# Shared-expert work of two mixture-of-experts layers moved behind the routing chain and behind the expert slots

## What is computed

```python
# first mixture
shared = silu(x @ shared_w1.T) @ shared_w2.T
gates, idx = top_k(x @ gate_w.T, 2); gates = softmax(gates)
out = shared + sum over the two experts of gate * (silu(x @ w1[e].T) @ w2[e].T)
# second mixture
w, idx = top_k(softmax(x @ w_router), 2); w = w / (sum(w) + 1e-8)
out = sum over the two of w * ((silu(x @ w_gate[e]) * (x @ w_up[e])) @ w_down[e])
      + (silu(x @ ws_gate) * (x @ ws_up)) @ ws_down
```

## Time and profile before

| | us |
|---|---|
| median of 3 runs | 769.45 (768.46 to 769.53) |
| the profiled execution, its own time | 768.8 |
| its span in the trace | 767.1 |
| TensorE busy | 582.7 (76% of the span) |
| VectorE busy | 422.9 (55%) |
| ScalarE busy | 333.4 (43%) |
| GpSimd busy | 352.9 (46%) |
| attention, up to the last rows normed | 0 to 79.5 |
| routing 1, up to the first turn of a slot | 79.5 to 118.8 |
| slots of layer 0 | 118.8 to 243 |
| combine, norm, state space | 243 to 545 |
| routing 2, up to the first turn of a slot | 545 to 604 |
| slots of layer 1 | 604 to 738 |
| combine, norm, store | 738 to 767.1 |

### The profile page before, as it was taken

One profiled execution on the slowest core, in us unless ns is written; L12 is line 12 of the kernel. 1 busy time (PEld: TensorE's weight loads), 2 busy tenths in 40 slices (PEclk: granted clock), 3 DMA queues, 4 the chain that ended last, 5 costly groups with the idle time before them and its releaser, 6 DMA issues.

```text
span 767.1 us, 9002 instructions
## 1 busy us (share of the span) xinstructions
PE 582.7 (76%) x2522; PEld 345.9 (45%) x2523; DVE 422.9 (55%) x717; ACT 333.4 (43%) x594; POOL 352.9 (46%) x281
## 2 busy tenths in 40 slices
PE   6887798788786539849776975665699799999940
PEld 3755475566564213214323332221355566666630
DVE  3344471000011869999999999999376233222326
ACT  3433332444444275764883685343212144433423
POOL 1000215666653116676667668576100456556422
PEclk9998699999999679998998998999989899999985
DMA  4503001111111943423443343342000101111123
GB/s 110 171 25 137 15 4 42 36 39 41 40 34 50 359 195 130 144 113 137 143 149 109 137 151 133 117 150 82 15 0 1 32 29 41 35 38 33 31 81 92
DMA packets 35135, 65.61 MB, mean 86 GB/s; under 512 B 6111, under 2 KB 23207, under 8 KB 34464
## 3 DMA queue, kind: packets, MB, share of 16 engines
q1 hardware_dynamic: 29824, 51.19, 19.7%
q0 software_dynamic: 4992, 9.32, 4.6%
q10 hardware_dynamic: 288, 4.72, 1.6%
HBM read 57.60 MB, written 8.52 MB: 86 GB/s over the span
## 4 chain that ended last, share of the span: by engine, by line
PE 41%; issue 16%; POOL 14%; DVE 13%; another core or an unknown queue 6%; ACT 6%; DMA 3%; SPq 0%; POOLq 0%; ACTq 0%; DVEq 0%
PE ps L600 8%; PE ps L581 8%; DVE wide L1352 7%; POOL wide L1475 6%; POOL w L1475 6%; PE ps L583 4%; PE ps L537 3%; PE ps L592 3%; PE ps L693 3%; ACT work L937 3%; PE ps L502 2%; PE ps L506 2%; PE ps L507 2%; PE ps L635 1%
## 5 line engine op out<-in xcount | busy, mean ns | idle before, releaser
L1352 DVE TENSOR_TENSOR_SCAN wide<-work,ps 128x1024 f32<-128x1024 f32 x64 | 146.2, 2284 | 1.9
L937 ACT ACTIVATE work<-work,a_neg 128x512 f32<-128x512 f32 (+1 forms) x128 | 84.5, 712 | 103.2 <-DVE wide L1352 83.1
L1504 POOL DMA_INDIRECT y_choice<-yout,dest x78 | 78.8, 1011 | 98.3 <-ACT yout L758 71.9
L1475 POOL TENSOR_TENSOR wide<-wide,w 128x1024 f32<-128x1024 f32 x32 | 75.6, 2362 | 62.0 <-DVE wide L1352 62.0
L693 PE MATMUL ps<-w,ident 128*128 128x512 f32 x128 | 68.9, 669 | 33.4 <-POOL w L1475 33.4
L1475 POOL TENSOR_TENSOR w<-wide,w 128x1024 f32<-128x1024 f32 x32 | 78.4, 2454 | 32.0 <-DVE wide L1352 32.0
L1198 DVE COPY xT<-ps 128x128 f32<-128x128 f32 x78 | 22.7, 291 | 118.5 <-PE ps L575 62.3
L1345 DVE TENSOR_TENSOR ps<-ps,w 128x1024 f32<-128x1024 f32 x64 | 78.9, 1233 | 6.4
L693 PE MATMUL ps<-wide,ident 128*128 128x512 f32 x128 | 63.2, 617 | 21.5 <-POOL wide L1475 21.5
L1498 POOL DMA_INDIRECT xin<-xn_rows,source x40 | 39.2, 979 | 85.9 <-DVE dest L1173 74.3
L1203 DVE TENSOR_TENSOR wide<-wide,ps 128x512 f32<-128x512 f32 x39 | 26.8, 688 | 77.1 <-ACT wide L836 72.2
(11 more groups left out here) (234 smaller groups left out, 965.9 us busy)
## 6 DMA issues: line engine op xcount, KB each, us to landing
w<-bc_rows SPq DMA_DIRECT2D x64, 512.0 KB, 3.6
w<-in_w ACTq DMA_DIRECT2D x2, 2304.0 KB, 9.0
w<-y_choice SPq DMA_DIRECT2D x16, 256.0 KB, 3.7
wg<-in_wg SPq DMA_DIRECT2D x1, 2304.0 KB, 10.8
wu<-in_wu SPq DMA_DIRECT2D x1, 2304.0 KB, 15.8
wd<-in_wd SPq DMA_DIRECT2D x1, 2304.0 KB, 21.1
y_choice<-yout,dest POOLq DMA_INDIRECT x78
work<-in_x SPq DMA_DIRECT2D x4, 256.0 KB, 3.3
```

The source lines that it names most:

```text
L937: last = A(dA[j % 2][:, h, lo:S], delta[:, h, lo:S], ACT.Exp, scale=a_neg[:, j + h * NS:j + h * NS + 1])
L1352: V.tensor_tensor_scan(st[j % 2].rearrange("p h t -> p (h t)"), dA[j % 2].rearrange("p h t -> p (h t)"), dbu.rearrange("p h t -> p (h t)") ...
L1475: G.tensor_tensor(hc[j % 4], st[j % 2], bc_all[j % 4][:, S:2 * S].unsqueeze(1).to_broadcast([P, EH, S]), ALU.mult).then_inc(hc_set, 1)
L1504: G.indirect_dma_start(out=y_choice, out_offset=bass.IndirectOffsetOnAxis(ap=dest[:, y:y + 1], axis=0), in_=yout[y % 4][:, :], in_offset=N ...
```

## The change

1. **TensorE, layer 0.** `router` is split into `turn_rows` and `score_rows`. Blocks 0 to 2 of batch 0's `shared_up` (into banks 0 to 2) come before the last batch's turn, block 3 between turn and scores, blocks 0 to 2 of batch 1 before `counts`. `shared_down(2)` and `shared_down(3)` go behind the slots, after the state space block's tap matmuls.
2. **TensorE, layer 1.** Three blocks of batch 0 before the last turn, one before `counts`, then batch 1, down of 0, two blocks of batch 2, `table`, down of 1. Blocks 10 to 15 and `shared_down(2)`, `shared_down(3)` go behind the slots. The slots wait for `base_set` of batch 1 alone.
3. **VectorE.** `routing` becomes one uninterrupted chain. `top_two` works on a range of tiles: the first 12 tiles are done before the last batch's scores come, the last 4 after. `mask` is laid out expert first, so that the copies `L1116` and `L1117` go: the scan, a subtraction and an addition read PSUM themselves. `take_logits` and `reuse` of batch 2 move behind the last batch's statistics. `add_base(2)` and `add_base(3)` move behind the slots.
4. **GpSimd.** `shared_mult` of layer 1 moves from VectorE to GpSimd, ten blocks ahead of the first fetch and six behind the last store, ahead of `inverse_group`. It cannot read the up half in PSUM: ScalarE copies it to `ga` after each silu, and `gate_set` is raised after that copy.
5. **ScalarE** follows that order. Its silu table is loaded before the last turn's copy in layer 0, and two of the four blocks of batch 0 in layer 1 come before `apply_norm` instead of four.

```diff
+            pe.wait_ge(ld_f0, 32)
+            shared_up(0, 0, (0, 1, 2))
+            turn_rows(0, NB - 1)
+            shared_up(0, 0, (3,))
+            score_rows(0, NB - 1)
...
                 if l == 0:
-                    shared_up(0, 0)
-                shared_up(l, 1, (0, 1))
+                    shared_up(l, 1, (0, 1, 2))
+                else:
+                    shared_up(l, 0, (3,))
                 counts()
-                shared_up(l, 1, (2, 3))
-                shared_down(0)
-                shared_up(l, 2)
-                shared_down(1)
-                shared_up(l, 3)
-                table()
-                shared_down(2)
-                shared_down(3)
+                shared_up(l, 1, (3,) if l == 0 else range(HB))
+                shared_down(l, 0)
+                if l == 0:
+                    shared_up(l, 2)
+                    shared_down(l, 1)
+                    table()
+                    shared_up(l, 3)
+                else:
+                    shared_up(l, 2, (0, 1))
+                    table()
+                    shared_down(l, 1)
                 pe.wait_ge(*expert_set[l].at(1))
-                pe.wait_ge(*base_set[l].at(NB))
+                pe.wait_ge(*counts_taken[l].at(1))
+                pe.wait_ge(*base_set[l].at(2))
+                if l:
+                    pe.wait_ge(*gate_set[1].at(2 * HB + 2))
+                else:
+                    pe.wait_ge(*sT_set[0].at(NB * HB))
...
-            pe.wait_ge(a_set, 2)
+            pe.wait_ge(*hT_set[0].at(ROUTED))
+            shared_down(0, 2)
+            pe.wait_ge(bias_set, 1)
+            shared_down(0, 3)
...
-            shared_up(1, 0)
+            shared_up(1, 0, (0, 1, 2))
             turn_normed(NB - 1)
             route_out(NB - 1)
             moe(1)
+            shared_up(1, 2, (2, 3))
+            shared_down(1, 2)
+            shared_up(1, 3)
+            shared_down(1, 3)
...
-                        A(th[j % 2], bank(4 + j % 2), ACT.Silu).then_inc(gate_set[1].sem, 1)
+                        A(th[j % 2], bank(4 + j % 2), ACT.Silu)
+                        cp(ga[j % 2], bank(6 + j % 2)).then_inc(gate_set[1].sem, 1)
...
-            shared_silu(1, 0)
+            shared_silu(1, 0, (0, 1))
             apply_norm(NB - 1)
             router(1, NB - 1, LOOSE[0])
+            shared_silu(1, 0, (2, 3))
             moe(1)
+            act.wait_ge(*hs_set[1].at(ROUTED))
+            shared_silu(1, 2, (2, 3))
+            shared_silu(1, 3)
             for b in range(NB):
                 last_norm(b)
...
+            attend_norm(NB - 1, last_but_one)
+            dve.wait_ge(*logits_set[0].at(NB - 1))
+            top_two(0, EARLY)
             take_logits(0, NB - 1)
...
-                    link(V.tensor_copy(tot[:, :, :], tiles_ps.rearrange("p (t e) -> p e t", e=NE)))
-                    V.tensor_copy(pos[:, :, :].rearrange("p t e -> p (t e)"), before_ps).then_inc(counts_taken[l].sem, 1)
...
+                routing()
+                add_base(l, 0)
+                add_base(l, 1)
+                gating()
                 slot_steps(dve.Fori(0, LOOP_TRIPS), step)
                 if l:
                     for b in range(NB):
+                        if b >= 2:
+                            add_base(l, b)
                         combine(l, b)
                         variances(l, b)
                         if b:
                             pull_mean(l, b - 1)
...
+            def shared_mult(b, blocks=range(HB)):
+                for j in blocks:
+                    pool.wait_ge(*gate_set[1].at(b * HB + j + 1))
+                    if b >= 2:
+                        pool.wait_ge(*sy_ps[1].at(b - 1))
+                    G.tensor_tensor(sT[b % 2][:, j, :], th[j % 2], ga[j % 2], ALU.mult).then_inc(sT_set[1].sem, 1)
...
             moe(1)
+            shared_mult(2, (2, 3))
+            shared_mult(3)
             for g in range(NB):
                 inverse_group(1, g)
```

More of the change, by code:

```diff
@@ L146, in build @@
         ms = [sb(f"ms{k}", [P, NT]) for k in range(2)]
-        mask = sb("mask", [P, NT, NE])
+        mask = sb("mask", [P, NE, NT])
         gap = sb("gap", [P, NT]); egap = sb("egap", [P, NT]); den = sb("den", [P, NT]); zsum = sb("zsum", [P, NT])
@@ L631, in convolve @@
                     pe.wait_ge(bias_set, 1)
+                if x == 0 and h == 1:
+                    pe.wait_ge(*base_set[0].at(NB))
                 if h == 1 and x >= 2:
@@ L803, in _, with shared_silu @@
             attend(NB - 1, False, True)
-            router(0, NB - 1)
-            def shared_silu(l, b):
-                for j in range(HB):
+            def shared_silu(l, b, blocks=range(HB)):
+                for j in blocks:
                     n = b * HB + j
@@ L850, in step @@
                         cp(yout[q][:, :], bank(1, D)).then_inc(yout_set[l].sem, 1)
-                for b in range(l, NB):
-                    shared_silu(l, b)
+                shared_silu(l, 1)
+                shared_silu(l, 2, (0, 1) if l else range(HB))
                 exp_gaps()
+                if l:
+                    act.wait_ge(*sT_set[1].at(2 * HB + 2))
+                else:
+                    shared_silu(l, 3)
                 slot_steps(act.Fori(0, LOOP_TRIPS), step)
@@ L1025, in reuse, with attend_norm @@
                 dve.wait_ge(*kept[l].at(b + 1))
-            def attend_norm(b):
+            def attend_norm(b, between=lambda: None):
                 dve.wait_ge(ctx_ps, b * QT + QT)
@@ L1035, in attend_norm @@
                 norm_stats(lambda ins: ins.then_inc(stats_set[0].sem, 1))
+                between()
                 norm_apply(0, b)
@@ L1048, in attend @@
                     attend_norm(b - 1)
-                    take_logits(0, b - 1)
-                    reuse(0, b - 1)
+                    if not final:
+                        take_logits(0, b - 1)
+                        reuse(0, b - 1)
                 dve.wait_ge(probs_set, b * QT + QT)
@@ L1186, in routing @@
                     link(V.tensor_tensor(gates[1][:, :], gates[0][:, :], egap[:, :], ALU.mult))
-                    yield
-                route = routing()
                 def step(m, k):
@@ L1249, in moe, with add_base @@
                     pull_mean(l, NB - 1)
+            def add_base(l, b):
+                dve.wait_ge(*sy_ps[l].at(b + 1))
+                dve.wait_ge(*(normed_set if l else kept)[l].at(b + 1))
+                V.tensor_tensor(tiles(base[l][:, b * S:(b + 1) * S]), x_seq(b), tiles(bank(2 + b % 2)),
+                                ALU.add).then_inc(base_set[l].sem, 1)
             def combine(l, b):
@@ L1491, in moe @@
                     diagonals()
+                else:
+                    shared_mult(0)
+                    shared_mult(1)
+                    shared_mult(2, (0, 1))
                 pool.wait_ge(*idx_set[l].at(1))
```

179 lines of the change are left out of this document (77 added, 102 removed).

## The result

The changed kernel takes **746.93 us** (median of 4 runs, 744.96 to 747.80), the kernel before on the same chip 769.13. The ratio is 0.9708, with a 95% interval of 0.9675 to 0.9742: 22.2 us less, where 36.2 were forecast. The time lies above the range of 728 to 744.

What follows compares the result with a forecast made beforehand. No engine is busy over 76% of the span, so the stages count: shared work stands ahead of the slots on TensorE. -16.9 - 28.1 + 8.8 = -36.2 against the median 769.45 gives 733.2 us, range 728 to 744.

Steps and rivals of the forecast that it cites:

- What GpSimd may do to VectorE: Layer 1's products on GpSimd beside VectorE's routing chain: no slowdown charged, though the skill's rule meant some 6 us less gain.
- Exclusion: Rival, 13%: five GpSimd products hold up VectorE's layer 1 chain, scan to one-hot grows by 6 us; 739 us.
- Layer 0, -16.9: Layer 0's routing up to the first slot turn: the turn comes at 101.9 instead of 118.77, 16.9 us earlier.
- The early pass: Top two of the first 12 tiles before the last batch's scores, in both layers; credited with 1.4 us in each.
- Between slots and states, 0: Two down groups and additions moved behind layer 0's slots are hidden in idle time and cost nothing.
- Layer 1, -28.1: Layer 1's routing up to the first slot turn: the turn comes at 575.9 instead of 603.96, 28.1 us earlier.
- Tail, +8.8: Behind layer 1's slots: last combination starts 8.8 us later, 6.7 without two clock losses, as VectorE waits for GpSimd's power.
- The loop hangs on GpSimd's DMAs: Rival, 12%: layer 0's slot loop has fixed length from the first fetch, which moves by 12.7, not 16.9; 737.4 us.
- GpSimd's products too slow: Rival, 3%: products over 2.6 us delay layer 1's first fetch and the tail; at 5 us each, 776 us.
- Clock where I don't expect it: Rival, 15%: low clock adds 1.75 us at layer 1's scores and 1.9 at one or two restarts; 736 to 739 us.

Runs made afterwards that it cites:

- e5: e1 with layer 1's constants count_up, group_no and slot_row copied to PSUM ahead of the chain and read there; 714.55 us, ratio 0.9669.
- memset kernel: The changed kernel with layer 1's shared products on GpSimd replaced by memsets of the same tile; 708.35 us, ratio 0.9578.
- e9: The changed kernel with GpSimd's four diagonal operations put behind four of its last stores in layer 0; 716.29 us, ratio 0.9696.
- e1: The changed kernel with GpSimd's diagonal operations moved from beside layer 0's top two to behind its ninth fetch; 716.19 us, ratio 0.9698.
- e10: e9 with the top two of all sixteen tiles in one pass behind the last logits, in both layers; 715.47 us, ratio 0.9691.
- e4: e1 with TensorE doing two more blocks in layer 0 before it waits for the last logits; 717.02 us, ratio 0.9703.
- e11: e8 with two extra matrix products into an unread bank in TensorE's gap ahead of layer 0's first slot turn; 735.28 us, ratio 0.9605.
- e7: e1 with all sixteen layer 1 products on VectorE out of PSUM, no ScalarE copies, TensorE's six tail blocks ahead of both down groups; 708.96 us, ratio 0.9593.
- e8: e7 with the diagonals placed as in e9, behind GpSimd's last stores; 709.22 us, ratio 0.9617.

## Why the prediction was wrong

**The step that failed** is the one under "What GpSimd may do to VectorE": "So I charge nothing for the products beside the routing chain". Products and diagonals hold VectorE up, and are held up. The rule of the Trainium skill that the forecast set against this step ("SBUF — State Buffer", Who interferes with whom) says that a VectorE operation with two inputs in SBUF contends with a GpSimd operation that reads SBUF, and not with one that only writes it. The trace agrees: 0.26 becomes 1.87 us, an operation with one input in PSUM keeps its 1.46, and a memset holds nothing. That the loser always waits for the whole of the other's operation is not what the rows show: behind a copy of 0.65 us `L1189` lost 0.29, and beside the three small diagonals no operation lost more than 0.05. By the same section a one-input `tensor_scalar` or cast of VectorE can contend too. This shows as well: `L1192` takes 1.55 beside products and 0.54 beside memsets, and the cast `L1188` 1.25 instead of 0.18 in `e5`. The forecast took as evidence against the rule a power on four elements a partition. The right pair was in the trace of before. VectorE's product of two SBUF inputs in the state space stage, alone and beside GpSimd's operations, and GpSimd's row:

```profile
282.57 1.23 DVE L1324 TENSOR_TENSOR ps<-work 128x1024 f32<-128x1024 f32 x1
...
343.42 2.10 DVE L1324 TENSOR_TENSOR ps<-work 128x1024 f32<-128x1024 f32 x1
```

```profile
342.07 5.65 POOL L1475 TENSOR_TENSOR w<-wide,w 128x1024 f32<-128x1024 f32 x2
```

1.23 becomes 2.10, and two operations of 2.36 take 5.65. The rival *Exclusion*, at 13% and 739 us, had the mechanism and, for layer 1 up to `dest`, the size: it said 6, the memset kernel shows 6.0 (37.98 against 31.96). That the size fits is in part luck, for the rival put all 6 between scan and one-hot, where 4.1 were, and 2.1 lay ahead of the scan. It missed that the diagonals do the same in layer 0. About 6.2 us of the 12.3 by which the measured sum of the stages falls short are these holds in layer 1, and about 2.4 are the diagonals' holds in layer 0 with the late copy and the low clock that came with them (`e9`, whose rows are normed at the same time, has its first turn at 103.97, the changed kernel at 106.41). With them charged the sum would have been about 742.

By the steps of the forecast:

- *Layer 0, -16.9, measured -12.4.* The mask was expected at 83.2 and came at 85.66: 2.1 us of holds in the early pass. TensorE waits for the copied logits before its next blocks, which I had not counted, idles 3.26 us, and their lower clock costs 1.7 (4.54 us for six matmuls instead of 2.84): scan at 88.03 instead of 83.95. The forecast let the first turn wait for silus and had no term for the landing of the fetched rows; it left 2.5 us between fetch and turn (99.4 to 101.9), and the turn came 2.83 after the fetch (103.58 to 106.41), released by the DMA. That `e1` had its first turn at 101.65 does not confirm the sum of the steps. It is luck: its rows were normed 2.4 us before those of the first run (73.67 against 76.04). `e9`, normed at 76.06, had the turn at 103.97, so the steps were 2.1 us short even with the diagonals away: 0.84 at the scan, 0.84 more at the fetch, 0.39 more from the fetch to the turn.
- *The early pass*, which the forecast credited with 1.4 us in each layer, gave 1.14 in layer 1 and nothing in layer 0 (`e10`: 8.71 against 8.73 us from the normed rows to the scan).
- *Between slots and states, 0, measured +1.9.* The down groups are hidden, as said (6.92 us of idle time remain behind them, 12.79 before), and so are the additions. What grew is the wait for the reloaded rows, 5.10 us instead of 3.68, and the convolutions, 10.17 us instead of 9.54.
- *Layer 1, -28.1, measured -21.4.* The scan came 2.3 us late, 2.1 of it from holds (memset kernel: 15.67 against 17.75), scan to one-hot took 4.1 more, the way from `dest` to the turn 0.5 more. The scores at full clock (1.06) were right. TensorE's queue, which was to hold the table for 1.4 us, didn't, as the one-hot came later than the queue; in the memset kernel, without holds, it did, by 1.3 us, and there `dest` came at 31.96 where the forecast had 31.9.
- *Tail, +8.8, measured +6.9.* Two clock losses of 1.9 were charged and neither came in that run: 3.84 us a down group. What is left is the forecast's own 6.7 without losses, so the path was right and the charge for the clock was not. The hold of 2.0 us on the combination (4.32 against 2.31) is no term of the tail: it fills time in which VectorE would have waited for the power anyway. The memset kernel has no hold there (2.31), stalls 2.73 for the power and ends only 1.5 us sooner, which two memsets in place of two products on the path to the sixteenth explain (0.52 instead of 1.27 each). In `e1` one of the losses did come, 5.47 us for the first down group behind 2.51 us of idle time; its tail is 8.6 longer than the one before.
- *The loop hangs on GpSimd's DMAs* is false: fetch and turn moved by 8.6 and 12.4, and the slots kept their length.
- *GpSimd's products too slow* is false: 1.27 us.
- *Clock where I don't expect it* is true in kind (1.7 us ahead of the counts, a place that was not foreseen). `e1`, `e4`, `e9` and `e10`, each 1.8 to 2.4 us faster from the normed rows to the first turn, all end within 1.5 us of the changed kernel. Low clock stands at the places where they lose it again (start of the slots, state space stage, tail); that it is the cause there is argued from the rows, and no experiment moved it.

## What to carry to other kernels

Before moving work to an idle GpSimd, find a row of the old trace where it reads as many elements beside a VectorE operation of the kind that will be its neighbour; if both read SBUF, count the moved work as serial with VectorE. A product whose second input lies in PSUM was cheaper left on VectorE (0.6 us) than moved to GpSimd (1.27 us, a copy of 0.6 on ScalarE, and the holds). A gain at one stage is to be read at the end of the next ones as well, and from an instruction just ahead of the edit, not from the start of the trace: of 3.8 us at the first slot 1.6 were there before the edited code began, and the other 2.2 were gone at the last instruction.

## What had not been expected

- The changed kernel takes 24 us more in layer 0's slots on one chip than on another (123.6 and 99.7 us), 4.4 more in layer 1's, and 2 more in all the rest. The cause wasn't looked for.
- TensorE's granted clock was low behind idle times of 3.26 us and 2.81 us, but also behind 0.57 (`e4`) and 0.22 (`e11`). Behind the same gaps it fell in one run and not in another: ahead of layer 0's slots (1.08 us, 0.69 and then 0.50, in the changed kernel's first run; 1.17 us, 1.00, in its run beside `e5`), and in the tail (2.51 us, a down group of 5.47 in `e1` and of 3.84 in the changed kernel). In `e1`, `e7`, `e8` it fell in the state space stage in the same stretch, 340 to 375 us, in the changed kernel hardly.
- Attention, which is the same code in all these runs, has its last rows normed from 73.2 to 73.9 us on in `e1` and `e5` to `e8` and from 75.3 to 76.1 in the other eight runs of a kernel with the change. Between 62 and 70 us the granted clock is 1.00 in `e1` and 0.79 in the changed kernel.
